# One float32 product for three float32r products, with scores on 32-row tiles and gated sums on three engines

## The reference

```python
Q = (x @ Wq.T).reshape(H, b, s, dkh)   # H = 16 heads, dkh = 16
K = (x @ Wk.T).reshape(H, b, s, dkh)
V = (x @ Wv.T).reshape(H, b, s, dvh)
scores = jnp.einsum('hbqd,hbkd->hbqk', Q, K)
atten = jax.nn.softmax(scores, axis=-1)
out = jnp.einsum('hbqk,hbkd->hbqd', atten, V).reshape(b, s, -1)
y = out + x                            # then normalised over axes 1 and 2
...
for e in range(E):                     # E = 8 experts, top 2 by gate
    h = xt @ w_in[e].T                 # HIDDEN = 1024
    y = y + gates[:, e:e + 1] * (h @ w_out[e].T)
```

## Time and profile before

| | |
|---|---|
| median of 3 runs | 1052.1 us (1048.34 to 1052.39) |
| profiled execution | 1055.4 us |
| its span, first to last instruction | 1053.6 us |
| mean granted TensorE clock | 0.981 of 2.4 GHz |
| busy: TensorE, VectorE, ScalarE, GpSimd | 1012.4, 873.8, 627.3, 78.7 us |
| instructions | 20712 |
| DMA | 108.58 MB, mean 103 GB/s |

### The profile page before, as it was taken

The page is one execution under the profiler, slowest core; times in us unless marked ns, Lnnn a source line. Parts: engine busy times, 40 slices in busy tenths (PEclk is TensorE's granted clock), DMA queues, the critical chain, the costliest instruction groups (busy, mean ns, idle before and its releaser), DMA issues.

```text
span 1053.6 us, 20712 instructions
## 1 busy us (share of the span) xinstructions
PE 1012.4 (96%) x7816; PEld 527.1 (50%) x7816; DVE 873.8 (83%) x1255; ACT 627.3 (60%) x1231; POOL 78.7 (7%) x205
## 2 busy tenths in 40 slices
PE   6778999999999999999999999999999999999995
PEld 6666888888886533333333333333333333333332
DVE  4301777877877989999999999999999999999976
ACT  2100111111110178888888888888888888888885
POOL 2100111011100001000100010001000100010001
PEclk9899999999999989999999999999999999999998
DMA  7777456445555012222222222222222222222214
GB/s 274 271 246 223 130 161 181 129 133 158 144 162 160 5 52 62 71 61 70 62 70 62 69 61 69 62 70 61 70 62 71 60 70 61 71 60 71 63 25 160
DMA packets 127042, 108.58 MB, mean 103 GB/s; under 512 B 81120, under 2 KB 102368, under 8 KB 126944
## 3 DMA queue, kind: packets, MB, share of 16 engines
q1 hardware_dynamic: 114016, 86.03, 29.6%
q10 hardware_dynamic: 12928, 21.24, 5.9%
HBM read 80.75 MB, written 42.21 MB: 117 GB/s over the span
## 4 chain that ended last, share of the span: by engine, by line
PE 89%; DVE 5%; DMA 4%; issue 1%; SPq 0%; ACT 0%; ACTq 0%; POOL 0%; POOLq 0%; DVEq 0%
PE ps L892 27%; PE ps L874 22%; PE ps L829 15%; PE ps L862 11%; PE ps L801 5%; PE ps L775 3%; DMA wp<-w_out_t 3%; PE ps L790 2%; PE ps L903 2%; DVE negm L620 1%; PE ps L915 1%; DVE acc L608 1%; PE ps L763 1%; DVE xnc L733 0%; DMA qf<-ot 0%
## 5 line engine op out<-in xcount | busy, mean ns | idle before, releaser
L620 DVE TENSOR_REDUCE negm<-ps 128x1 f32<-128x1024 f32 x512 | 618.5, 1222 | 31.9 <-PE ps L862 15.3
L464 ACT ACTIVATE wp<-ps 128x512 f32<-128x512 f32 x684 | 369.4, 602 | 88.7 <-PE ps L874 62.6
L874 PE MATMUL ps<-qf,kf 50*128 50x512 f32 x1024 | 388.1, 455 | 2.1 <-DVE ps L679 1.7
L862 PE MATMUL ps<-kf,qf 48*128 48x512 f32 x1024 | 368.1, 451 | 0.2 <-DVE negm L620 0.2
L874 PEld LDWEIGHTS ps<-qf,kf 50*128 50x128 f32 x1024 | 160.5, 186 | 207.4 <-ACT wp L464 107.7
L892 PE MATMUL ps<-wp,vb 128*17 128x256 f32 x2736 | 215.7, 387 | 0.3 <-issue 0.3
L862 PEld LDWEIGHTS ps<-kf,qf 48*128 48x128 f32 x1024 | 146.3, 186 | 7.5 <-issue 5.7
L464 ACT ACTIVATE vstage<-ps 128x512 f32<-128x512 f32 x170 | 102.3, 602 | 24.6 <-PE ps L874 11.2
L829 PE MATMUL ps<-mth,xth 128*128 128x512 f32 x256 | 103.8, 405 | 3.4 <-DVE spare L552 2.4
L892 PEld LDWEIGHTS ps<-wp,vb 128*17 128x17 f32 x2736 | 46.9, 95 | 118.5 <-ACT picks L464 42.8
L464 ACT ACTIVATE picks<-ps 128x512 f32<-128x512 f32 x170 | 102.4, 602 | 0.0
(11 more groups left out here) (104 smaller groups left out, 675.9 us busy)
## 6 DMA issues: line engine op xcount, KB each, us to landing
feat_d<-qk_d SPq DMA_DIRECT2D x64, 256.0 KB, 4.5
qf<-feat_d SPq DMA_DIRECT2D x128, 128.0 KB
wp<-w_in SPq DMA_DIRECT2D x16, 512.0 KB, 4.3
wp<-w_out_t SPq DMA_DIRECT2D x16, 512.0 KB, 5.2
qk_d<-stage ACTq DMA_DIRECT2D x32, 256.0 KB
qk_d<-spare ACTq DMA_DIRECT2D x32, 256.0 KB
qf<-feat_d SPq DMA_DIRECT2D x128, 64.0 KB
kf<-feat_d SPq DMA_DIRECT2D x128, 64.0 KB
```

Source lines behind the costliest of these rows:

```text
L464: nc.scalar.activation(weight_tile(n, j, b)[:, h * HALF:(h + 1) * HALF], ps[:, ST_BANK[(2 * unit + b) % 3], :], ACT.Exp).then_inc(exp_done, 1)
L620: nc.vector.tensor_reduce(negm[:, n % 2, qt:qt + 1], ps[:, b:b + 2, :].rearrange("p b c -> p (b c)"), AX.X, ALU.max, negate=True).then_inc ...
L862: last = nc.tensor.matmul(ps[:, MAX_BANK[turn % 2] + half, :], qf[rows, u, qt * P:(qt + 1) * P], kf[rows, u, :], start=True, stop=True)
L874: nc.tensor.matmul(ps[:, ST_BANK[(2 * unit + half) % 3], :], kf[rows, u, j * P:(j + 1) * P], qf[rows, u, h * HALF:(h + 1) * HALF], start=T ...
```

## The change

Products are made once in plain float32. The float32r tiles, their low parts and the operations for them go. `y_bank` has 2 products a bank, 8 a tile (line 832 after); a projection has 2 products per output in place of 6. The features are stored once (16 rows) and copied to four groups of 32 rows: groups 0 and 1 serve the maxima, groups 2 and 3 the scores, where row 16 holds the maximum. Four products of a unit thus lie in four row tiles. TensorE turns the maxima to rows directly.

The gated sums are split: VectorE takes banks 0 and 1, ScalarE scales banks 2 and 3 into `scaled_by` (line 442 after), GpSimd adds (`add_scaled`). Weights have six slots in place of two, four of them in `wp` and two in `qf`. Chunks 0 and 1 are projected among the composites; chunks 2 to 7 among the expert sums. Stores of values, queries and keys are issued by SyncE, and each head's regrouping is a transfer of its own, eight heads ahead. Gates are worked out for two chunks at a time. The early maxima are crossed with the last 8 tiles, two a tile.

```diff
-    TERMS = 3
-    FR = DH * TERMS
-    SR = FR + 2
-    ROWS = P // 2
+    GROUP = 32
+    GROUPS = P // GROUP
+    FR = DH
+    SR = FR + 1
...
         def feature_loads(n):
 
-            for half in range(2):
-                first = half * ROWS
-                keys = slice(half * HALF, (half + 1) * HALF)
-                yield (qf, slice(first, first + 2 * DH), slice(0, POS),
-                       feat_d[n, 0, 0].unsqueeze(0).to_broadcast([2, DH, POS]))
...
+            for group in range(GROUPS):
+                rows = slice(group * GROUP, group * GROUP + DH)
+                keys = slice(group % 2 * HALF, (group % 2 + 1) * HALF)
+                yield qf, rows, slice(0, POS), feat_d[n, 0]
+                yield kf, rows, slice(0, HALF), feat_d[n, 1, :, keys]
...
+            def add_scaled(t):
+                par, tile = t % 2, acc[:, bass.ds(t, 1), :].rearrange("p o d -> p (o d)")
+                for j in range(E // 2 - BY_VECTOR):
+                    pool.wait_ge(ff_scaled[j], 2 * (t + 1))
+                nc.gpsimd.tensor_tensor(scaled_by[:, par, 0:2], scaled_by[:, par, 0:2], scaled_by[:, par, 2:4], ALU.add
+                                        ).then_inc(ff_step, 1)
...
+                nc.gpsimd.tensor_tensor(tile, tile, vsum[:, par], ALU.add).then_inc(ff_sum, 1)
...
+            def scale_experts(t, j):
...
+                act.wait_ge(y_ready[j], t + 1)
+                for h in range(2):
+                    nc.scalar.activation(scaled_by[:, t % 2, 2 * (j - BY_VECTOR) + h, :], ps[:, Y_BANK[j], h * D:(h + 1) * D],
+                                         ACT.Copy, scale=gates[:, t, 2 * j + h:2 * j + h + 1]
+                                         ).then_inc(ff_scaled[j - BY_VECTOR], 1)
...
             def y_bank(t, j):
-                p, tokens = t // TC % 2, slice(t % TC * P, (t % TC + 1) * P)
-                pe.wait_ge(ff_added[j], 2 * t)
-                products = [(v, m, kt) for kt in range(KT) for v, m in ((xth, mth), (xth, mtl), (xtl, mth))]
...
+                if t and j < BY_VECTOR:
+                    pe.wait_ge(ff_added[j], 2 * t)
+                elif t:
+                    pe.wait_ge(ff_scaled[j - BY_VECTOR], 2 * t)
...
+                for kt in range(KT):
+                    last = nc.tensor.matmul(ps[:, Y_BANK[j], :], xt[:, t // TC % SETS, kt, tokens],
+                                            mt[:, kt, 2 * j:2 * j + 2, :].rearrange("p e d -> p (e d)"),
+                                            start=kt == 0, stop=kt == KT - 1)
...
             def max_scores(n, qt, halves=(0, 1)):
...
-                    rows = half_rows(half, FR)
+                    rows = group_rows(half, FR)
...
-                rows = half_rows(half, SR)
+                rows = group_rows(GROUPS // 2 + half, SR)
...
             def maxima_to_rows(n):
-                pe.wait_ge(msplit, 2 * (n + 1))
-                source = mpart[:, n % 2].bitcast(FP32).rearrange("p w q -> p (w q)")
+                pe.wait_ge(turn_done, max_turn[n, NKT - 1] + 1)
+                source = negm[:, n % 2]
```

More of the change, by code:

```diff
@@ L261, in regroup @@
[L261 to L268, removed]
+                    sp.dma_start(half[slot], w.rearrange("e h d -> (e h) d")[rows, :]
+                                 .rearrange("(p h) d -> p h d", h=HU)).then_inc(w_in_s[slot], 16)
@@ L278, in _ @@
                     load_weights(e, h)
+            for c in range(PAIR):
+                values_out(c)
+                qk_out(c)
             def features(n):
@@ L372, in residual @@
                                         att[:], ALU.add).then_inc(y_done, 1)
[L374 to L381, removed]
+            for t in range(NT):
+                add_scaled(t)
+            for pair in range(NB // 2 - 1):
+                residual(pair)
             def batch_rstd(part, entries):
@@ new lines, in second_weight, with qk_copy @@
+            def second_weight(pair):
+                act.wait_ge(gap_done, pair + 1)
+                rows = slice(PAIR * TC * pair, PAIR * TC * (pair + 1))
+                nc.scalar.activation(ex[:, rows], gap[:, rows], ACT.Exp).then_inc(gexp_done, 1)
+            def qk_copy(c, o):
+                if o == 0 and c >= 2:
+                    act.wait_ge(qk_stored[c % 2], 64 * (c // 2))
+                act.wait_ge(project_ready, 2 * TC * c + TC + o + 1)
+                nc.scalar.copy(stage[:, c % 2, o, :], ps[:, PROJECT_BANK[o % 2], :]).then_inc(qk_evac, 1)
@@ new lines, in add_experts @@
+                if j == 0 and t >= 2:
+                    dve.wait_ge(ff_sum, t - 1)
+                dve.wait_ge(y_ready[j], t + 1)
+                for h, total in enumerate((tile, vsum[:, t % 2])):
+                    product = ps[:, Y_BANK[j], h * D:(h + 1) * D]
+                    gate = gates[:, t, 2 * j + h:2 * j + h + 1]
+                    if j:
+                        dve.wait_ge(ff_added[j - 1], 2 * t + h + 1)
+                    if j == 0 and h == 1:
+                        nc.vector.tensor_scalar(total, product, gate, None, ALU.mult).then_inc(ff_added[j], 1)
+                    else:
+                        nc.vector.scalar_tensor_tensor(out=total, in0=product, scalar=gate, in1=total,
+                                                       op0=ALU.mult, op1=ALU.add).then_inc(ff_added[j], 1)
@@ L674, in _ @@
[L674 to L682 removed]
+            for c in range(PAIR + 1):
+                layernorm(c)
@@ L848, in half_rows @@
-            def half_rows(half, last):
-                return slice(half * ROWS, half * ROWS + last)
+            expert_product(1, 1)
+            for o in range(2, 4):
+                project_qk(0, o)
+            expert_product(2, 0)
+            transposes(1)
+            expert_product(2, 1)
+            for t in range(TC):
+                project_v(1, t)
+            expert_product(3, 0)
+            for o in range(2):
+                project_qk(1, o)
+            expert_product(3, 1)
@@ new lines, in _ @@
+            pe.wait_ge(m_done, KT * E)
+            for t in range(NT - 2 * TC):
+                c, i = t // TC + PAIR, t % TC
+                for j in range(E // 2):
+                    if c < NC:
+                        if i == 0 and j == 0:
+                            transposes(c)
+                        elif i == 1:
+                            project_v(c, j)
+                        elif i >= 2 and j % 2 == 0:
+                            project_qk(c, 2 * (i - 2) + j // 2)
+                    y_bank(t, j)
```

515 lines of the change are left out of this document (234 added, 281 removed).

## The result

The changed kernel takes 2001.8 us (median of 4 runs, 2001.3 to 2002.3), the kernel before 1052.2 beside it: a ratio of 1.903, 95% interval 1.897 to 1.909. I had forecast 1352 (1290 to 1430), so the direction was right and the size far off.

A forecast was written before the change was run, and what follows sets the result against it. TensorE, busy in 96% of the span, was taken as the bound. Composites 92, expert sums 310, attention loop 936 and end 18 sum to 1356 against the profiled 1055.4, hence forecast 1352 us, range 1290 to 1430.

The forecast's parts named there:

- The clock is 0.99 and more in both later stages, so I take 0.858.: Expert sums and attention loop: clock stays near full, so a float32 product of 512 columns costs 0.858 us.
- upper price of the product, 1.10: Float32 product of 512 columns priced from a slow block at clock 0.86 to 0.93: 1.10 us, not taken.
- A product: 0.858: One float32 product of 512 columns is two records of 0.429 us, replacing three float32r products of 0.696 together.
- Composites 92: First stage, before the expert sums: from 99.9 to 92 us, a change of -8, bounds 85 and 99.
- 14.5 + 5.3: Composites: more weight slots save 14.5 us of waits for weights and 5.3 of slow blocks behind them.
- Four row tiles side by side in one round: Attention loop: all four products of a unit run together in one round of 0.858 us.
- The estimate of 1485: Total of about 1485 us if four row tiles give 3.07x, not 4x, making the score round 1.12.
- The exponential's lag: Attention loop: the fourth product waits 0.18 us for an exponential, 0.09 a unit on average, making the unit 1.74.
- 1.65: Attention loop: length of one unit in us before the exponential's lag is added.
- 936: Attention loop: 32 pairs of heads at 29.2 us each, 936 in place of 675.6, a change of +260.
- The gated sums are worth nothing: Expert sums: moving gated sums off VectorE gains nothing, as its 205 us of work was no bound.
- Rivals 1 to 4: Staircase of records 1966 us (7%); only two tiles together 1808 (6%); one-record float32 product 988 (3%); loop unchanged 1092 (2%).

The follow-up runs named there:

- e1: The changed kernel with its products of scores and maxima reading all 32 rows of each row tile, in place of 17 and 16: 1318.3 us.
- e7: The kernel before with four weight slots in place of two, the added two in the half of `xn` filled later: 1039.5 us, ratio 0.9865.
- e8: The kernel of e1 with half of every exponential left out (256 of the 512 queries done): 1286.6 us.
- e3: The changed kernel with 32 rows read for the maxima alone, the scores staying at 17: 1324.7 us (two runs, 1318.4 and 1331.0).
- e6: The kernel of e1 with zeros in the key rows beyond the seventeenth: 1319.5 us.
- e9: The changed kernel with 32 rows read for the scores alone, the maxima staying at 16: 1319.2 us.
- e4: The kernel before with one float32r term in place of three in its scores (16 and 18 rows), loads cut to match: 1512.3 us.

## Why the prediction was wrong

By its own steps:

- *"The clock is 0.99 and more in both later stages, so I take 0.858."* This is the step that failed: the clock that the sum and the range put on the loop. I read the clock of the loop off a loop whose products use 48 and 50 rows a tile, and carried it to one with 16 and 17. TensorE's being busy was my only ground, and it was as busy after as before. The loop at half clock is 1585.0, at full clock (e1) 904.0: 681 us of the 949 that the change costs. None of my rivals had it, and the range had no room for it: I had used the lower clock only as an upper price of the product, 1.10, and left it out. Why the chip lowers the clock here is not shown; what is shown is that reading all 32 rows in either half of the products keeps it up.
- *A product: 0.858.* Right at the full clock: 512 records of `y_bank` (the page's L832), six of which last 2.74 in the timeline (from 201.81), 0.43 each without the tail of 0.17; stage 308.2 against 310. The expert sums cost 46 more; I had 48.
- *Composites 92.* Right: 89.8, and 88.6 in e1. e7 shows the gain of the weight slots alone: 14.2, with the clock restored as part of it, where my terms have 14.5 + 5.3 = 19.8. The 6.5 of waits for low parts, which the changed kernel does not have, cover the difference.
- *Four row tiles side by side in one round.* Right: rows at 1060.85 to 1060.87 at the lower clock, 712.19 to 712.21 at the higher. The estimate of 1485, with 1.12 for the stream, falls too: from 712.19 to the sums at 713.26 it is 1.07, with the weight load and the change to column tiles in it. "TensorE: Matmul & The Clock Gate", Part 3, in the Trainium skill has matmuls start strictly in program order. Taken record by record, as I took it, the traces here do not agree, for column tiles and now for row tiles, since a tile's second record is passed by the first records of three other tiles. Taken product by product they do: the four first records start in the order of the products (1060.85 to 1060.87), and so do the second ones.
- *The exponential's lag.* Right in kind (e8), 0.06 where I had 0.09. With 1.63 where I had 1.65 that is 0.05 a unit, 26 of the 32 by which the loop of e1 is shorter (904 for 936), and the loop is most of 1318 for 1352.
- *The gated sums are worth nothing.* Consistent: VectorE went from 205 busy us in that stage to 87, and the stage grew by TensorE's products alone. GpSimd's additions took 1.27 and three times 0.72 a tile, 3.4 where I had 3.7; ScalarE's scaling 0.47. It was not tried alone.
- *Rivals 1 to 4* fall: the starts of the records are not a staircase, four tiles share one round, a product has two records, and the loop did not stay at 676.

The account of the 949: composites -10, expert sums +46, loop at full clock +228 (904.0 - 675.6), clock +681. About 4 are left: the end is 1.3 longer, and the profiled execution before was 3 above its median.

"TensorE: Matmul & The Clock Gate", Part 1, in the Trainium skill has the clock follow how busy TensorE has been. Taken as the busy time of the profile, the trace does not agree: TensorE is busy for 1584.94 of 1585.03 us at clock 0.50. e1, e3, e6 and e9 show that the rows read by the products belong to it, and the last two heads of e3 that what ran before does.

## What to carry to other kernels

Before costing a matmul that uses fewer rows of the array, ask what the granted clock will be, not only how many columns it streams. A kernel can be 100% busy on TensorE at half its speed, and of the profile's columns only the clock shows it. If small products are needed, let them read the whole row tile, with zeros in the spare rows of one operand: here it cost no time of its own and gave 683 us back, and half of the products were enough. Look at where the clock falls, too: here that was at the start of a stage, and it did not come back before the scores ended. And a total that fits a rival is no evidence for it; the starts of the records are.

## What the runs showed of the hardware

- Reading spare rows that are zero in the key tile keeps the clock up as well as reading numbers: 1319.5 against 1318.3 us, where 16 and 17 rows gave 2001.8.
- In the loop, rounds of 96 to 128 rows had the full clock; rounds of 34 rows in float32r (e4) and of 66 in float32 had the half.
- The same 197 records of TensorE, with rounds of 34 rows, took 27.95 us at 1.00 in e3 and 49.30 us at 0.50 in the changed kernel: the level that they came in with was kept.
- When the last scores of the changed kernel are done, the sums over values (128 rows, 17 columns on each of four column tiles) run alone, and the mean clock of that stretch is 0.70, so the higher level came back for a part of it:

```profile
1984.00:1988.00 4.00, 3.50 (x42) 1.43 (x35) 0.00 (x0) 1.11 (x3) 0.00 (x0) 0.70 0.00 0
```

- A float32r product of 16 or 18 rows at half clock (a unit of 2.13) is slower than one of 48 and 50 rows at the full clock (1.22): three terms were cheaper than one.
